# The weights' rests of a Mamba in-projection, subtracted by GpSimd instead of VectorE

## The reference, cut to what matters

```python
h = _L0_tok_ref(x, W, b)                       # patches @ W.T + b
h = concatenate([h, _L0_txt_ref(x_txt, emb)], axis=1)   # rows of a word table, gathered
# L0_attn_ref(_layernorm(h)):
xn = _layernorm(x, ln1_w, ln1_b)               # x is already normalised once
zxbcdt = u @ in_w                              # 192 x 806, for each of two directions
z, xBC, dt = ...                               # then convolution, scan, gate, ...
```

## Time and profile before

| | us |
|---|---|
| time, median of 3 runs | 735.59 (735.18 to 738.79) |
| the profiled execution | 735.96 |
| its span, first to last instruction | 734.2 |
| PE busy in the span | 636.1 (87%) |
| VectorE busy | 490.3 (67%) |
| ScalarE busy | 380.9 (52%) |
| GpSimd busy | 276.9 (38%) |

### The profile page before, as it was taken

One profiled execution on the slowest core, in us unless ns is written; L12 is line 12 of the kernel. 1 busy time (PEld: TensorE's weight loads), 2 busy tenths in 40 slices (PEclk: granted clock), 3 DMA queues, 4 the chain that ended last, 5 costly groups with the idle time before them and its releaser, 6 DMA issues.

```text
span 734.2 us, 13415 instructions
## 1 busy us (share of the span) xinstructions
PE 636.1 (87%) x4912; PEld 567.9 (77%) x4912; DVE 490.3 (67%) x1267; ACT 380.9 (52%) x872; POOL 276.9 (38%) x292
## 2 busy tenths in 40 slices
PE   3669899899899556478999999798999999999993
PEld 2659776579898433267888888798999999999993
DVE  3768688774604877747777783497477778677761
ACT  1349876863433466545655543342255656556541
POOL 5340526444201424043223326001434657566633
PEclk9959999999999757579999999799999999999997
DMA  6500000224000670300000002103275866768733
GB/s 181 118 1 5 1 1 1 99 63 132 1 0 1 160 136 0 119 0 5 4 4 5 6 3 87 48 1 119 63 269 148 259 224 206 260 169 262 194 98 69
DMA packets 27585, 64.67 MB, mean 88 GB/s; under 512 B 5951, under 2 KB 19152, under 8 KB 25184
## 3 DMA queue, kind: packets, MB, share of 16 engines
q0 software_dynamic: 12640, 46.90, 21.5%
q1 hardware_dynamic: 13116, 16.04, 8.1%
q10 hardware_dynamic: 1764, 0.88, 0.4%
HBM read 58.55 MB, written 5.74 MB: 88 GB/s over the span
## 4 chain that ended last, share of the span: by engine, by line
PE 47%; DVE 6%; ACT 2%; issue 2%; POOL 1%; POOLq 0%; DVEq 0%; ACTq 0%
PE bank L1911 10%; PE bank L1871 4%; PE bank L1874 4%; PE bank L1875 4%; PE bank L1873 4%; PE bank L1872 4%; PE bank L1791 3%; PE bank L1727 2%; PE bank L1770 2%; DVE amx L2521 1%; PE bank L1747 1%; PE bank L1777 1%; PE bank L1689 1%; PE bank L1753 1%; DVE big L2527 1%
## 5 line engine op out<-in xcount | busy, mean ns | idle before, releaser
L2596 DVE TENSOR_SCALAR big<-bank 128x256 f32<-128x256 f32 (+1 forms) x126 | 52.0, 412 | 54.8 <-PE bank L1875 54.6
L1305 ACT ACTIVATE big<-bank 128x256 f32<-128x256 f32 (+1 forms) x126 | 47.6, 379 | 49.6 <-PE bank L1875 49.6
L801 POOL TENSOR_TENSOR big<-big,arc 128x423 f32<-128x423 f32 (+1 forms) x48 | 37.8, 814 | 77.5 <-DVE arc L2541 77.5
L828 POOL DMA_INDIRECT total<-big,goal x32 | 54.2, 1692 | 24.5 <-issue 18.0
L1871 PE MATMUL bank<-x_lead,w_lead 128*128 128x256 f32 x192 | 56.5, 294 | 0.5 <-issue 0.5
L1874 PE MATMUL bank<-x_both,w_lead 128*128 128x256 f32 x192 | 54.5, 284 | 0.0
L1875 PE MATMUL bank<-x_both,w_rest 128*128 128x256 f32 x192 | 54.2, 282 | 0.0
L1873 PE MATMUL bank<-x_lead,w_rest 128*128 128x256 f32 x192 | 54.1, 282 | 0.0
L1872 PE MATMUL bank<-x_rest,w_lead 128*128 128x256 f32 x192 | 53.9, 281 | 0.0
L2607 DVE SCALAR_TENSOR_TENSOR big<-big 128x256 f32<-128x256 f32 (+1 forms) x126 | 50.1, 409 | 0.0
L835 POOL DMA_INDIRECT big<-x_rows,origin x32 | 33.6, 1051 | 41.1 <-DVE goal L2653 23.2
(11 more groups left out here) (544 smaller groups left out, 2009.9 us busy)
## 6 DMA issues: line engine op xcount, KB each, us to landing
big<-in_patches SPq DMA_DIRECT2D x2, 768.0 KB, 8.9
areg<-in_e_gate_up SPq DMA_DIRECT2D x1, 1536.0 KB, 6.6
shared_lead<-in_e_gate_up POOLq DMA_DIRECT2D x1, 1536.0 KB, 7.1
wreg<-in_ffn_w SPq DMA_DIRECT2D x1, 1152.0 KB
ffw_lead<-in_ffn_w POOLq DMA_DIRECT2D x1, 1152.0 KB, 7.0
out<-total SPq DMA_DIRECT2D x2, 423.0 KB
wreg<-in_in_w SPq DMA_DIRECT2D x2, 419.0 KB
wreg<-in_in_w SPq DMA_DIRECT2D x4, 209.5 KB
```

Of the source, the lines that this page charges most:

```text
L828: pool.indirect_dma_start(out=total, in_=YS[:, j % 2, q * D:(q + 1) * D], in_offset=None, out_offset=bass.IndirectOffsetOnAxis(ap=goal[:, ...
L1305: nc.scalar.activation(GS[:, n % 3, 0:w], bank[2 * (n % 2)][:, 0:w], ACT.Silu).then_inc(S["g_silu"], 1)
L2596: v.tensor_scalar(UM[:, n % 3, 0:w], bank[2 * (n % 2) + 1][:, 0:w], 10.0, -10.0, ALU.min, ALU.max).then_inc(S["u_clip"], 1)
```

## The change

The four subtractions leave VectorE's stream and stand in GpSimd's, right behind its gathers and ahead of its wait for the last transposes. GpSimd waits for `in_lead` where VectorE did. Operands, areas and semaphores are the same.

```diff
@@ gpsimd
                 pool.indirect_dma_start(out=words[:, t, :], out_offset=None, in_=i["emb"],
                                         in_offset=bass.IndirectOffsetOnAxis(ap=ids[:, t:t + 1], axis=0))\
                     .then_inc(gathered[t // 3], 16)
+            for d in range(2):
+                cols = slice(d * DCOLS, d * DCOLS + WCOLS)
+                pool.wait_ge(S["in_lead"], 2 * d + 2)
+                pool.tensor_tensor(INL[:, cols], in_full[:, cols], INH[:, cols], ALU.subtract).then_inc(S["in_rest"], 1)
+                pool.tensor_tensor(INBL[:, cols], in_both[:, cols], INBH[:, cols], ALU.subtract).then_inc(S["in_rest"], 1)
+
             pool.wait_ge(ln_turned, 3)
@@ vector
-            def weight_rests(d):
-
-                cols = slice(d * DCOLS, d * DCOLS + WCOLS)
-                dve.wait_ge(S["in_lead"], 2 * d + 2)
-                v.tensor_tensor(INL[:, cols], in_full[:, cols], INH[:, cols], ALU.subtract).then_inc(S["in_rest"], 1)
-                v.tensor_tensor(INBL[:, cols], in_both[:, cols], INBH[:, cols], ALU.subtract).then_inc(S["in_rest"], 1)
-
             image(2)
             together(0)
             image(3)
             twice_normal(0)
-            weight_rests(0)
             together(1)
             first_rests(0)
             twice_normal(1)
             together(2)
-            weight_rests(1)
             first_rests(1)
             twice_normal(2)
```

## The result

| | before | after |
|---|---|---|
| time, median of 11 runs, us | 735.59 (733.86 to 738.79) | 740.83 (738.63 to 743.71) |
| profiled execution | 735.96 | 738.63 |
| its span | 734.2 | 736.9 |
| VectorE, XS 0: start and end | 30.25, 31.21 | 30.79, 36.62 |
| VectorE, XS 2: end | 43.90 | 48.20 |

The ratio is 1.0062 with a 95% interval of 1.0049 to 1.0075: slower by 4.6 us (3.6 to 5.5); the two medians lie 5.2 apart. The profiled execution is the fastest of the 11, so its span shows less than the medians do.

What follows compares the result with a forecast made beforehand. VectorE, without an idle row from 30.25 to 43.9 us, was taken to set the stage's pace. GpSimd's lock on XS 0 makes XS 2 4.1 us later, passed on one for one: 735.59 to 739.7 us, range 734.6 to 741.8.

Steps and rivals of the forecast that it cites:

- The best case by counting VectorE's time: Stage from 30 to 49 us: no lock, XS 2 ends 1.78 us earlier, 733.8 or less; chance 0.09.
- The turns with GpSimd: At XS 0, rows alternate with whole GpSimd subtractions, so it ends 5.27 us later; full turns give 739.7, chance 0.48.
- The rival in which only the first rests are held: XS 0 not locked, only VectorE ops with two SBUF operands; XS 2 0.2 us early, 735.4; chance 0.14.
- The 0.07 us of margin at 30.18: GpSimd's second subtraction starts at 30.18, 0.07 us before XS 0 at 30.25, and so has the turn.
- The rival that GpSimd loses the turn: At 30.18 XS 0 goes first, turns only in part: 736.4 to 737.9 us; chance 0.22.
- The price of the turns: At XS 0, a GpSimd subtraction ends 1.82 us after VectorE's end, an XS row 0.23 after GpSimd's end.
- The chain behind XS 0: After XS 0, PE and ScalarE set the pace; XS 2 ends at 48.00 instead of 43.90, 4.1 us later.
- The clock's part: Group 0's transposes at 1.2 GHz after PE's idle: ScalarE starts 1.52 us later instead of 0.91, 0.6 us of the 4.1.
- One for one to the end: From the end of XS 2 on, a shift of the stage reaches the kernel's end undiminished, 4.1 us.
- the sign that the prediction named: The sum is wrong if the shift at 48 us and that of the span differ by over 1 us.
- The clock rival: PE's return to 2.4 GHz, around 55 us, comes later against the work: up to 2 us more, beyond 741.8; chance 0.07.
- the line that I had put at 739.3: Whole kernel: measurement tells no change within about 0.5%, 3.7 us, so slower begins at 739.3; chance of slower 0.38.

Runs made afterwards that it cites:

- e3: The change, with XS 0 computed as scalar_tensor_tensor with one SBUF and one PSUM operand; ratio 0.9990 to the kernel before.
- e1: The change, with GpSimd's four subtractions held back until VectorE's three rows of XS 0 are done; ratio 1.0033 to the kernel before.
- e4: Half of the change: only the first pair of subtractions on GpSimd, the second at its old place on VectorE; ratio 1.0000 to the kernel before.
- e5: Kernel before, with first pair on GpSimd, XS 0 using a PSUM operand, second pair in VectorE's idle time behind XS 2; ratio 0.9990.
- e7: Kernel before plus four GpSimd memsets of 128x846 into unused memory, subtractions staying on VectorE; ratio 1.0003.
- e10: Repeat on another chip: kernel before with the second pair of subtractions moved behind XS 2 on VectorE; ratio 0.9995.
- e12: Repeat on another chip: kernel before with one subtraction on GpSimd ahead of XS 0, second pair late on VectorE; ratio 0.9992.
- e8: Kernel before, with all four subtractions and three filler additions on VectorE ahead of XS 0, no GpSimd work added; ratio 1.0076.
- e9: The kernel before, unchanged, measured again against itself on a third chip; ratio 0.9990.
- e2: Kernel before, with the second pair of subtractions still on VectorE but moved to its idle time behind XS 2; ratio 0.9985.

## Why the prediction was right

- **The best case by counting VectorE's time (1.78 us less)** did not come, as the prediction had it; no run reached it.
- **The turns with GpSimd.** Right, in the form given: XS 0 is held whole instructions at a time (1.98, 2.00, 2.00 us; I gave 1.5 to 2.3 each). e3 shows that the form decides, e1 that the first rests would have been held as well, e4 that one row is held per subtraction. That XS belongs to the forms that are held, which no row of before showed, is now shown. The rival in which only the first rests are held is refuted with it.
- **The 0.07 us of margin at 30.18.** XS 0 came at 30.79 and GpSimd's second subtraction at 30.71: both 0.54 later, the order the same. In e4 (30.87 and 30.79) again. The order was less of a chance than the margin suggests: both starts count from ScalarE's casts, 27.02 here and 26.48 before, and move together. Where ScalarE had to wait for VectorE's statistics behind the casts (e5 to e7, e10 to e12), XS 0 started at 31.6 to 32.1; the change was not profiled with such an entry. The rival that GpSimd loses the turn did not occur in any profile.
- **The price of the turns** was mis-sized by a little: 2.05 us a turn, measured 1.92, because GpSimd does not slow at all for a row of 0.37 (1.95 to 1.97 each). So XS 0 took 5.83 and not 6.23. Behind a row of 0.55 with two operands GpSimd did take 2.26 (e1, e3), as the rows of before had it.
- **The chain behind XS 0.** XS 2 ended 4.30 later than in the profile of before; I gave 4.1. Of the 4.30, 0.54 are the later entry, which I had not forecast, and 3.76 the stage, where the turns came 0.4 cheaper than I had them. That 4.30 lies so near to 4.1 is luck: the two misses offset each other. The clock's part is as worked out: from the transposes to ScalarE's start 1.57 instead of 0.91.
- **One for one to the end.** Within the error of the runs for a lateness of this size: 4.6 us (3.6 to 5.5) for 3.8 to 4.3, and e8 agrees. It fails in the profiled pair, where the shift is 4.3 at 49.86 (GpSimd's memset, 45.56 before) but 2.7 at the end. By the sign that the prediction named (shift and span within 1 us) its sum is wrong there. Part of the way can be followed on GpSimd's rows. The shift is still 3.1 at 80.02 (76.96 before) and 3.0 at 87.92 (84.88 before), 1.45 at 97.20 (95.75 before) and 1.45 at its load of the feed-forward weights (168.72, line 733 before at 167.27). Between 80 and 100 us the execution of before had a granted clock of 0.91 to 0.92, and the changed one 1.00. In e1, whose granted clock from 80 to 110 us is 0.94 like before's, the shift of 3.2 at the same memset is 3.5 at that load. So the clock's course in one execution can take off about 1.5 us of shift. What took 1.2 off between 50 and 77 us, and put 1.2 on behind 169 us, is open.
- **The clock rival**, up to 2 us on top. The rise to 1.00 did come later: 0.54 in the microsecond from 55 where before had 1.00. No loss of this size shows, as the shift fell and did not grow from 50 to 77 us.
- **The size.** 739.7 forecast, 740.83 measured (735.59 plus the 4.6 of the ratio is 740.2): past the line that I had put at 739.3. I had given 0.38 to slower and 0.58 to no change that can be told, so the case that I called likeliest came, and the outcome that I gave most weight did not.

One for one is not shown for small shifts of the stage: e4 and e7 lengthened it by 1.0 and 1.2 us and moved no time that the runs can tell. Their intervals reach to 1.0 and 1.2 us, so they do not refute it either; in e9 one kernel differed by 0.1% from itself.

## What to carry to other kernels

An engine with 18.7 us free is not free for its neighbour: before elementwise work goes to GpSimd, list what VectorE does in those microseconds and in which form; here tensor_scalar from SBUF to SBUF, and tensor_tensor with two SBUF operands, waited for whole GpSimd subtractions (1.98 and 2.13 us for 0.37 and 0.55), while rows with one SBUF and one PSUM operand (1.06 for three) and statistics (0.88 for three) kept their times. A short instruction pays the most for its size: each row of 0.37 us here waited for one of 1.96, so three rows grew by 4.9 us, more than the 3.7 us of work that had been moved away. Where the work has to be there, change the form of what it meets (e3 took the whole loss back), or use idle time of VectorE itself (e2: 0.5 and, repeated, 0.2 us off the stage; no gain in time that holds in both).

## What the hardware showed that I had not expected

- GpSimd's subtractions did not grow for VectorE's rows of 0.37 (1.95 to 1.97 us with and without), although each row ended 0.11 to 0.12 us behind a subtraction and the next subtraction had begun; they grew by 0.3 us behind a row of 0.55 us with two SBUF operands.
- GpSimd's memsets, which read nothing, held tensor_scalar as well: rows of 1.00 and 0.93 us for 0.37, beside memsets of 0.80 to 0.91 us.
- A stage 5 us later raised the time by 5.7 us (4.3 to 7.0), one 1 us longer by nothing that twelve runs could tell.
